# Top-2 mixture of experts behind a recurrent attention layer: combining, second normalisation and output by block instead of in a pass of their own

## The chip, the core and the metric

One core of a Trainium2 chip runs the whole kernel. The metric is the device time of one execution in microseconds (us): the median over several runs.

## The reference

`x` has two sequences of 2048 tokens with 256 channels, 4096 tokens in all.

```python
xx = pad(x, one step)[:, :-1, :]
k, v, r = (x*m + xx*(1-m)) @ W            # one m and W for each
a = (sigmoid(r) * wkv(decay, first, k, v)) @ Wo   # a scan over time in each channel
x1 = layernorm(x + a)
logits = x1 @ Wg + bg                     # 8 experts
s, e = top_k(logits, 2);  s = softmax(s)
h = act_e(x1 @ W1[e] + b1[e])             # 1024 wide; gelu for even e, silu for odd e
out = layernorm(x1 + sum over the two picks of s * (h @ W2[e] + b2[e]))
```

`wkv` keeps two running sums and a running maximum, so that exponentials stay bounded. All is fp32.

## The kernel before

The kernel is written engine by engine in Bass: each engine (PE, ACT, DVE, POOL, and SP for loads and stores) has a program of its own, and semaphores tie them together. An engine runs its instructions in the order in which they are written, so this order is what decides. Products of fp32 matrices are made as three products of a high and a low half ("h" and "l" in names).

**Attention stage.** Eight chunks of 256 time steps for both sequences (512 tokens, four groups of 128 rows). Each engine's `step(i)` works on several chunks: DVE scans chunk i, ACT makes its exponents (`exponents`, L885 to L890, `bonuses`, L895), and normalises chunk i-1 (`normalise_x1`, L933), for which POOL's `spread_of(i-1)` (four operations, L563 to L568) has made scale and shift. The router's choice is made by DVE in `choose` (maxima and their places, L1117 to L1130) and `place` (the slot of each pick in its expert's region, L1188 to L1199). POOL's `send_records` writes each token's record (x1 and two numbers, 258 floats) into `records_dram` twice, by eight indirect DMAs (L583), for chunk i-3, and ahead of `spread_of(i-1)`. SP stores x1 to `x1_dram`.

**Block stage.** The 8192 records lie in order of experts. They are worked through in blocks of 256 rows; for these inputs there are 35 in use, of at most 39. In step t, PE turns block t+2 (L823), makes product 1 of block t+1 into the four PSUM tiles `hT_ps` (L800) and product 2 of block t into `y_ps` (L809). ACT applies gelu or silu with the bias in place, writes the high half `aTh` and loads the records of a later block. DVE adds b2 (`y_sb`, L1299), makes the halves of x, the destination (`dest`, L1309) and the lower half `aTl` quarter by quarter (L1323). PE's product 1 of the block after next writes a quarter of `hT_ps` only when its `aTl` is done. POOL scatters the results by token and pick into `expert_out_dram` (L618, two a block). When the last block of expert e-2 is done it splits the weights of expert e from `staging` into `wx`: L533 rounds to the high half, L535 subtracts for the low half. Expert 1 is split before the first block.

**Last stage.** For 16 pieces of 128 time steps of both sequences, SP loads both picks' results of each token, DVE and ACT weigh and add them to x1, DVE makes mean and variance, POOL scale and shift (L634 to L639), ACT normalises (L1032), and SP stores to `out`.

A wait is written with a step's number: `t.upto(n)` stands for n increments in every step up to t, `t.upto(n, k)` for n in every step before t and k in step t; `after(engine, semaphore, value)` is left out where the value isn't positive. `t.slot` is the step's buffer in its ring.

Of the kernel before, what the change touches and what calls it, by code (L numbers as in the profile page):

```python
# [82 lines left out]
def build(nc, x, decay, first, mix_k, mix_v, mix_r, wkT, wvT, wrT, woT, w1, b1, w2, b2, wgT, bg, out):  # L83
# [18 lines left out]
    REC = C + 2  # L102
# [3 lines left out]
    PIECES = T // P  # L106
    RING = 4
    W1E, W2E = CC * F, FC * C
# [6 lines left out]
    ys = nc.dram_tensor("expert_out_dram", (2 * TOKENS, C), F32, kind="Internal").ap()  # L115
    x1d = nc.dram_tensor("x1_dram", (B, T, C), F32, kind="Internal").ap()

    with ExitStack() as ctx:
# [24 lines left out]
        top2 = sb("top2", [P, NCH, J, 2])  # L143
        score = sb("score", [P, NCH * J, 2])
        score_t = sb("score_t", [P, NCH * J, 2])
# [74 lines left out]
        slot_f = sb("slot_f", [P, J, 2], F32, phase_a)  # L220
        slot_i = [sb(f"slot_i{n}", [P, J * 2], I32, phase_a) for n in range(RECS)]
# [16 lines left out]
        xx = sb("xx", [P, PIECES, B, C])  # L238
# [3 lines left out]
        dest = [sb(f"dest{n}", [P, BH], I32, phase_b) for n in range(RING)]  # L242
# [4 lines left out]
        y_sb = [sb(f"y_sb{n}", [P, BH, C], F32, phase_b) for n in range(RING)]  # L247
# [4 lines left out]
        yy = [sb(f"yy{n}", [P, B, 2 * C]) for n in range(RING)]  # L252
        zz = [sb(f"zz{n}", [P, B, C]) for n in range(RING)]
        res = [sb(f"res{n}", [P, B, C]) for n in range(RING)]
        y2 = [sb(f"y2_{n}", [P, B, C]) for n in range(RING)]
        stats_c = [sb(f"stats_c{n}", [P, B, 6]) for n in range(RING)]
        mv_c = [sb(f"mv_c{n}", [P, B, 2]) for n in range(RING)]
        rstd_c = [sb(f"rstd_c{n}", [P, B]) for n in range(RING)]
        shift_c = [sb(f"shift_c{n}", [P, B]) for n in range(RING)]

# [3 lines left out]
        bias1_done, top2_done = sem("bias1_done"), sem("top2_done")  # L264
# [22 lines left out]
        x1_out = [sem(f"x1_out{n}") for n in range(RECS)]  # L287
# [6 lines left out]
        y_out = [sem(f"y_out{n}") for n in range(RING)]  # L294
# [3 lines left out]
        mm2_done, y_done = [sem(f"mm2_done{n}") for n in range(BH)], sem("y_done")  # L298
        exp_done, score_done = sem("exp_done"), sem("score_done")
        yy_in = [sem(f"yy_in{n}") for n in range(RING)]  # L300
        res_out = [sem(f"res_out{n}") for n in range(RING)]
        xx_in, y2_done, c_sum2 = sem("xx_in"), sem("y2_done"), sem("c_sum2")
        c_sum, c_bn, c_mv, c_var, c_rstd, c_res = (sem(n) for n in ("c_sum", "c_bn", "c_mv", "c_var", "c_rstd", "c_res"))

        REC_DMAS = 2 * J * 16
        ROUTE1, ROUTE2 = 2 * J + 3, 7
# [6 lines left out]
        def blocks_in_line(body):  # L313

            for n in range(-2, BLOCKS + 1):
                body(Step(None, n, RING, BLOCKS))

        LAST = ALWAYS // RING * RING

        def blocks(eng, body):  # L320

            plain = lambda n: Step(None, n, RING, BLOCKS)
            for n in range(-2, RING):
                body(plain(n))
            with eng.Fori(1, LAST // RING) as m:
                for n in range(RING):
                    body(Step(m, n, RING, BLOCKS, LAST // RING))
            for n in range(LAST, BLOCKS + 1):
                body(plain(n))
# [7 lines left out]

        def pieces(eng, body):

            for n in range(RING):  # L340
                body(Step(None, n, RING, PIECES))
            with eng.Fori(1, PIECES // RING) as m:
                for n in range(RING):
                    body(Step(m, n, RING, PIECES))

        def column(i, b, k):

            at = (i.off // TH * J + b * TH + i.off % TH) * 2 + k
            return at if i.fixed else i.m * (i.every // TH * J * 2) + at
# [15 lines left out]
        def store_chunk(sp, ap, i, rows, done):  # L365
            for b in range(B):
                sp.dma_start(ap[b, bass.ds(i.number * TC, TC), :].rearrange("(h p) c -> p h c", p=P), rows[:, b]).then_inc(done, 16)

# [9 lines left out]
        def kept(eng, c):  # L378

            after(eng, x1_out[c.number % RECS], c.number // RECS * B * 16)  # L380

        def phase_b_may_start(eng):
            eng.wait_ge(table_done, 1)
            for n in range(2):
                eng.wait_ge(dummy_out[n], 2 * 16)
            for n in range(RECS):
                eng.wait_ge(rec_out[n], users(n) * REC_DMAS)
                eng.wait_ge(x1_out[n], users(n) * B * 16)
# [17 lines left out]
        def _(sp):  # L406
# [26 lines left out]
            sp.wait_ge(padded, 3)  # L433
# [3 lines left out]
            def step(i):  # L437
# [24 lines left out]
            for e in range(2, E):  # L462
                sp.wait_ge(weights_ready, e)
                load_raw(e)
                if e == 2:
                    for b in range(B):
                        sp.dma_start(xx[:, :, b, :], x1d[b].rearrange("(q p) c -> p q c", p=P)).then_inc(xx_in, 16)
# [37 lines left out]
        def _(pool):  # L505
# [82 lines left out]
            def step(i):  # L588
# [6 lines left out]
                if (i - 1).exists:  # L595
                    spread_of(i - 1)
# [802 lines left out]
```

## Time and profile before

| | before |
|---|---|
| runs | 771.36, 774.31, 773.06 us; median 773.06 us |
| profiled execution | 775.2 us, its span 773.4 us |
| mean granted clock of TensorE | 0.907 |
| busy in the span: PE, DVE, ACT, POOL | 84%, 59%, 51%, 38% |
| longest groups: products L800 and L809 | 25% of the chain of waits each |
| DMA | 78.4 MB, 101 GB/s on average |

Times in the profile are microseconds from the span's start; a row of a timeline gives start, length, engine, line, operation, output and inputs, and in brackets how long the engine stood idle before it and what ended that. The chain of waits is followed back from the last instruction, at each step to what released it. Attention runs to about 290 us, blocks from there to 715 us, the last stage from there to the end.

### The profile page before, as it was taken

How to read it: one execution, taken by the hardware profiler on the slowest of the kernel's cores; microseconds unless marked ns; L12 is line 12 of the kernel's file. 1: busy time of each engine (PE TensorE's matmuls, PEld its weight loads, DVE VectorE, ACT ScalarE, POOL GpSimd, SP SyncE). 2: the span in 40 equal slices, each digit the busy share in tenths (PEclk: the TensorE clock that was granted, in tenths of full speed). 3: DMA queues.
4: the chain of work that ended last, by engine and by line, in shares of the span. 5: the costliest groups of instructions: out<-in, count | busy, mean ns of one | idle time of the engine just before them, and what ended most of it. 6: DMA issues, size and time to landing. Idle time of an engine off the chain costs nothing.

```text
span 773.4 us, 14741 instructions
## 1 busy us (share of the span) xinstructions
PE 648.2 (84%) x4512; PEld 605.9 (78%) x4512; DVE 453.3 (59%) x960; ACT 395.2 (51%) x717; POOL 295.3 (38%) x299
## 2 busy tenths in 40 slices
PE   4979799999976516999999999999999999999000
PEld 3858688788855416999999999999999999999000
DVE  3748889999996353844545345455464354442584
ACT  2545576576662103645546446456646546453374
POOL 4000116446555542525327263263461361212364
PEclk9998899999976657999999999999999999999555
DMA  8200221322122266661413214214141111201793
GB/s 262 80 28 1 81 82 56 111 81 99 67 75 97 91 176 206 198 228 39 152 51 115 86 43 151 58 33 153 50 159 49 39 46 43 57 12 34 232 309 123
DMA packets 56610, 78.39 MB, mean 101 GB/s; under 512 B 5174, under 2 KB 46083, under 8 KB 56356
## 3 DMA queue, kind: packets, MB, share of 16 engines
q1 hardware_dynamic: 40468, 50.54, 19.9%
q0 software_dynamic: 6496, 16.99, 6.3%
q10 hardware_dynamic: 9520, 9.25, 4.5%
q8 instruction: 71, 1.16, 0.6%
q14 instruction: 55, 0.45, 0.2%
HBM read 49.14 MB, written 28.40 MB: 100 GB/s over the span
## 4 chain that ended last, share of the span: by engine, by line
PE 73%; DVE 10%; issue 7%; ACT 3%; DMA 3%; POOL 2%; another core or an unknown queue 0%; SPq 0%; ACTq 0%; DVEq 0%; POOLq 0%
PE hT_ps L800 25%; PE y_ps L809 25%; PE vr_ps L670 8%; PE k_ps L670 7%; PE wo_ps L678 3%; PE xT_ps L823 2%; DVE o_all L1081 1%; DVE dest L1309 1%; PE small_ps L692 1%; POOL rstd_c L637 1%; PE xT_ps L661 1%; DVE xl L1159 1%; DMA yy<-expert_out_dram 1%; DMA records_dram<-rec,slot_i 1%; ACT res L1032 1%
## 5 line engine op out<-in xcount | busy, mean ns | idle before, releaser
L800 PE MATMUL hT_ps<-xTh,wx 128*128 128x256 f32 x1120 | 210.7, 286 | 0.4 <-issue 0.3
L809 PE MATMUL y_ps<-wx,aTh 128*128 128x256 f32 x1088 | 197.4, 283 | 0.9 <-DVE y_sb L1299 0.9
L800 PEld LDWEIGHTS hT_ps<-xTh,wx 128*128 128x128 f32 x1120 | 177.5, 192 | 1.3 <-issue 0.7
L1323 DVE TENSOR_TENSOR aTl<-hT_ps,aTh 128x512 fp32r<-128x512 f32 x140 | 93.3, 688 | 135.4 <-ACT aTh L991 135.4
L809 PEld LDWEIGHTS y_ps<-wx,aTh 128*128 128x128 f32 x1088 | 169.7, 192 | 1.1 <-issue 1.1
L618 POOL DMA_INDIRECT expert_out_dram<-y_sb,dest x70 | 68.3, 976 | 253.8 <-DVE y_sb L1299 239.0
L800 PE MATMUL hT_ps<-xTl,wx 128*128 128x256 f32 x560 | 158.7, 283 | 0.0
L809 PE MATMUL y_ps<-wx,aTl 128*128 128x256 f32 x544 | 154.0, 283 | 0.0
L985 ACT ACT_TABLE_LOAD x35 | 44.9, 1283 | 191.8 <-PE hT_ps L800 177.6
L985 ACT ACTIVATE hT_ps<-hT_ps,b_c 128x256 f32<-128x256 f32 x280 | 113.4, 469 | 0.8 <-PE hT_ps L800 0.3
L800 PEld LDWEIGHTS hT_ps<-xTl,wx 128*128 128x128 f32 x560 | 107.8, 192 | 0.0
L809 PEld LDWEIGHTS y_ps<-wx,aTl 128*128 128x128 f32 x544 | 104.4, 192 | 0.0
L583 POOL DMA_INDIRECT records_dram<-rec,slot_i x64 | 75.1, 1174 | 66.5 <-DVE rec L1199 40.6
L670 PE MATMUL vr_ps<-xh,wq 128*128 128x512 f32 x256 | 87.5, 414 | 0.0
L991 ACT ACTIVATE aTh<-hT_ps 128x512 fp32r<-128x512 f32 x140 | 84.2, 649 | 0.0
L1299 DVE TENSOR_TENSOR y_sb<-y_ps,b_b 128x256 f32<-128x256 f32 x70 | 29.4, 424 | 82.5 <-PE y_ps L809 81.2
L535 POOL TENSOR_TENSOR wx<-staging,wx 128x4096 fp32r<-128x4096 f32 x7 | 63.8, 9120 | 0.6
L670 PEld LDWEIGHTS vr_ps<-xh,wq 128*128 128x128 f32 x256 | 50.3, 197 | 11.8
L670 PE MATMUL k_ps<-xh,wq 128*128 128x512 f32 x128 | 48.0, 449 | 13.1 <-DVE nd L1088 11.1
L670 PE MATMUL vr_ps<-xl,wq 128*128 128x512 f32 x128 | 52.3, 408 | 0.0
L670 PEld LDWEIGHTS k_ps<-xh,wq 128*128 128x128 f32 x128 | 28.0, 219 | 21.1 <-issue 14.2
L678 PE MATMUL wo_ps<-wo,newton 128*128 128x256 f32 x128 | 34.9, 421 | 7.9 <-DVE newton L1109 4.4
(181 smaller groups left out, 870.0 us busy)
## 6 DMA issues: line engine op xcount, KB each, us to landing
staging<-in_L_ffn_W SPq DMA_DIRECT2D x16, 1024.0 KB
recs<-records_dram ACTq DMA_DIRECT2D x35, 258.0 KB
yy<-expert_out_dram SPq DMA_DIRECT2D x16, 512.0 KB, 5.3
xin<-in_L_attn_x SPq DMA_DIRECT2D x16, 256.0 KB, 4.4
xres<-in_L_attn_x SPq DMA_DIRECT2D x16, 256.0 KB, 3.0
x_dram<-rec SPq DMA_DIRECT2D x16, 256.0 KB, 3.3
xx<-x_dram SPq DMA_DIRECT2D x2, 2048.0 KB, 18.4
out<-res SPq DMA_DIRECT2D x16, 256.0 KB, 3.6
```

The costliest lines, as they stand in the source:

```text
L535: pool.tensor_tensor(wx[:, e % 2, 1, :], raw[:], wx[:, e % 2, 0, :].bitcast(F32), ALU.subtract).then_inc(weights_ready, 1)
L583: pool.indirect_dma_start(xs, bass.IndirectOffsetOnAxis(ap=slot_i[at][:, n:n + 1], axis=0), rec[at][:, j, :], None, bounds_check=DUMMY - 1 ...
L618: pool.indirect_dma_start(ys, bass.IndirectOffsetOnAxis(ap=dest[t.slot][:, h:h + 1], axis=0), y_sb[t.slot][:, h, :], None, bounds_check=2 ...
L670: ins = pe.matmul(out_ps.rearrange("p (b t) -> p b t", b=B), wq[:, mat, now, part, cc, oc * P:(oc + 1) * P], xpart[c.slot][:, cc, :, now:n ...
L678: ins = pe.matmul(wo_ps[:, h, :], mixed[:, cc, b, h * P:(h + 1) * P], wo[:, cc, :], start=cc == 0, stop=cc == CC - 1)
L800: ins = pe.matmul(hT_ps[b][:, f, :], wx[:, s, part, off:off + P], xpart[t.slot % 2][:, cc, :], start=k == 0, stop=k == len(terms) - 1)
L809: ins = pe.matmul(y_ps[h], apart[t.slot % 2][:, fc, h * P:(h + 1) * P], wx[:, s, part, off:off + C], start=k == 0, stop=k == len(terms) - 1)
L823: ins = pe.transpose(xT2_ps[:, cc, h * P:(h + 1) * P], recs[u.slot][:, h, cc * P:(cc + 1) * P], ident[:])
L985: act.activation(hT_ps[b][:, f, :], hT_ps[b][:, f, :], func, bias=b1_c[:, bass.ds(expert * FC + (2 * b + f), 1)]).then_inc(act_done, 1)
L991: act.activation(aTh[u.slot % 2][:, 2 * b - 2:2 * b, :], hT_ps[b - 1][:], ACT.Copy).then_inc(aTh_done, 1)
L1299: dve.tensor_tensor(y_sb[u.slot][:, h, :], y_ps[h], b2_b[:, bass.ds(expert * C, C)], ALU.add).then_inc(y_done, 1)
L1323: dve.tensor_tensor(aTl[u.slot % 2][:, 2 * b:2 * b + 2, :], hT_ps[b][:], aTh[u.slot % 2][:, 2 * b:2 * b + 2, :].bitcast(F32), ALU.subtract ...
```

## The change

The last stage is gone. Each record now carries all that its block needs: the token's number, the smaller and the larger of its two slots, two numbers that give the weight of either pick, and the smaller expert (262 floats). The weights come from POOL's new `compare` and `score_picks` and ACT's new `weigh` in the attention stage. A block's rows become `share = weight*(y + b2) + x1`, kept in SBUF and stored to `shares_dram`. For a row whose token had its other pick in an earlier block, that pick's share is fetched by an indirect load (`gather`); rows without one fetch nothing and read zeros. The weights are doubled, so the sum of both shares is twice the row to be normalised, and eps is taken times 4. The sum is normalised in the block stage and scattered to `out`, where rows that aren't the later pick have a number out of bounds. `shares_dram` and `other` are cleared first. x1 is neither stored nor reloaded. ACT's `normalise` is two Identity activations from `share` to `row_out`, and `store_shares` waits for `share_done` and issues one DMA of 256 KB.

```diff
@@ setup @@
-    REC = C + 2
+    REC = C + 6
+    KEEP = 6
+    MARKS = 8
-    ys = nc.dram_tensor("expert_out_dram", (2 * TOKENS, C), F32, kind="Internal").ap()
-    x1d = nc.dram_tensor("x1_dram", (B, T, C), F32, kind="Internal").ap()
+    us = nc.dram_tensor("shares_dram", (BLOCKS * BLK, C), F32, kind="Internal").ap()
@@ SP, step(i) of the attention stage @@
-                c = i - 2
-                if c.exists:
-                    store_chunk(sp, x1d, c, rec[c.number % RECS][:, :, 0:C].rearrange("p (b h) c -> p b h c", b=B), x1_out[c.number % RECS])
+                if i.exists:
+                    a, b = (BLOCKS * BH * n // NCH * P for n in (i.number, i.number + 1))
+                    sp.dma_start(us[a:b, :].rearrange("(n p) c -> p n c", p=P),
+                                 pad_rec[:, 0:C].unsqueeze(1).broadcast_to([P, (b - a) // P, C])).then_inc(shares_clear, 16)
@@ POOL, attention stage @@
+            def compare(c):
+                pool.wait_ge(route, c.upto(ROUTE1, 1 + 2 * J))
+                pool.tensor_tensor(gap[:], m8[:, :, 1], m8[:, :, 0], ALU.subtract).then_inc(gap_done, 1)
+                pool.wait_ge(later_done, c.upto(1))
+                pool.tensor_scalar(sign[:], later[:], -2.0, 1.0, ALU.mult, ALU.add).then_inc(gap_done, 1)
+            def score_picks(c):
+                at = c.number % RECS
+                pool.wait_ge(odds_done, c.upto(1))
+                pool.tensor_scalar(top_s[:], odds[:], 0.5, 0.5, ALU.mult, ALU.add).then_inc(score_done, 1)
+                pool.wait_ge(score_done, c.upto(7, 1))
+                pool.tensor_tensor(top_s[:], top_s[:], neg_one[:], ALU.pow).then_inc(score_done, 1)
...
             def send_records(c):
...
+                score_picks(c)
                 pool.wait_ge(label_done, c.upto(1))
+                pool.wait_ge(score_done, c.upto(7))
                 pool.wait_ge(x1_done, c.upto(J))
@@ POOL, step(i) @@
                 if early.exists and early.number < NCH - 3:
                     send_records(early)
+                if late.exists and late.number == NCH - 2:
+                    compare(late)
                 if (i - 1).exists:
                     spread_of(i - 1)
+                if late.exists and late.number != NCH - 2:
+                    compare(late)
@@ POOL, block stage @@
-            split(1)
+            def gather(t):
+                pool.wait_ge(where_done, t.upto(2))
+                if not t.fixed or t.number > 0:
+                    pool.wait_ge(share_out[(t.slot - 1) % RING], ring_count(t - 1, 16))
+                after(pool, sum_done, (t - RING).upto(1))
+                for h in range(BH):
+                    pool.indirect_dma_start(
+                        other[t.slot % RING][:, h, :], None, us,
...
             def scatter(t):
-                for e in range(2, E):
-                    with pool.If(end[e - 2] == t.number):
-                        split(e)
-                with if_used(pool, used, t):
-                    for h in range(BH):
-                        pool.wait_ge(y_done, t.upto(BH, h + 1))
-                        pool.indirect_dma_start(
...
+                pool.wait_ge(row_done, t.upto(BH))
+                for h in range(BH):
+                    pool.indirect_dma_start(
...
+                        row_out[t.slot % RING][:, h, :], None,
...
+            def block_step(t):
+                for stage, u in ((spread_z, t - 3), (gather, t - 1), (scatter, t - 4)):
+                    if u.exists:
+                        with if_used(pool, used, u):
+                            stage(u)
+                if t.exists and not (t.fixed and t.number == 0):
+                    for e in range(2, E):
+                        with pool.If(end[e - 2] == t.number):
+                            pool.wait_ge(share_done, (t - 1).upto(BH))
+                            split(e)
+            for n in range(MARKS):
+                block_step(Step(None, n, MARKS, BLOCKS))
+                if n == 1:
+                    split(1)
@@ PE, product 2 of block t @@
-                        after(pe, y_done, (t - 1).upto(BH))
+                        after(pe, share_done, (t - 1).upto(BH))
@@ ACT @@
+            def weigh(c):
+                act.wait_ge(gap_done, c.upto(2))
+                after(act, score_done, (c - 1).upto(7))
+                act.activation(odds[:], gap[:], ACT.Exp).then_inc(odds_done, 1)
@@ ACT, step(i), behind bonuses(i) @@
+                if (i - 3).exists and i.number < NCH:
+                    weigh(i - 3)
@@ ACT, block_step(t) @@
+                u = t - 4
+                        normalise(u)
                 u = t + 3
-                        after(act, txl_done, (u - RING).upto(1))
+                        after(act, share_done, (u - RING).upto(BH))
                         load_records(u)
...
+                u = t - 1
+                        store_shares(u)
@@ DVE, choose and place @@
+                dve.tensor_tensor(later[:], idxf[:, :, 1], idxf[:, :, 0], ALU.is_gt).then_inc(later_done, 1)
-                dve.tensor_copy(rec[c.number % RECS][:, :, C + 1:REC], slot_f[:, :, 1:2]).then_inc(slots, 1)
+                dve.tensor_tensor(rec[c.number % RECS][:, :, C + 1], slot_f[:, :, 0], slot_f[:, :, 1], ALU.min).then_inc(slots, 1)
...
@@ DVE, block stage @@
+            def shares(t):
...
+                    dve.tensor_tensor(y_ps[h], y_ps[h], b2_b[:, bass.ds(expert * C, C)], ALU.add).then_inc(y_done, 1)
+                    dve.scalar_tensor_tensor(out=share[at][:, h, :], in0=y_ps[h], scalar=weight[t.slot % 2][:, h:h + 1],
+                                             in1=recs[t.slot][:, h, 0:C], op0=ALU.mult, op1=ALU.add).then_inc(share_done, 1)
+            def add_other(t):
+                dve.wait_ge(other_in[t.slot], t.turn(16 * BH, 16 * BH))
+                dve.wait_ge(share_out[t.slot], t.turn(16, 16))
+                dve.tensor_tensor(share[at][:], share[at][:], other[t.slot][:], ALU.add).then_inc(sum_done, 1)
...
+                stages = [(shares, t - 1, ()), (halves, t + 2, ()), (add_other, t - 2, ()), (lower_quarter, t + 1, (0,)),
+                          (means, t - 2, ()), (mark, t, ()), (lower_quarter, t + 1, (1,)), (mark_more, t, ()),
+                          (lower_quarter, t + 1, (2,)), (mark_last, t, ()), (lower_quarter, t + 1, (3,))]
```

Three places where instructions move. DVE, one step of the block stage, before: the destinations (L1309) stand between the two halves of x, ahead of the four quarters of the lower half.

```order
L1299 TENSOR_TENSOR y_sb<-y_ps,b_b 128x256 x2
L336 COMPARE_AND_BRANCH
L1306 CAST xTh<-xT_ps 128x512
L1309 SCALAR_TENSOR_TENSOR dest<-recs,own_f 128x1 x2
L1314 TENSOR_TENSOR xTl<-xT_ps,xTh 128x512
L1303 UNCONDITIONAL_BRANCH
L336 COMPARE_AND_BRANCH
L1323 TENSOR_TENSOR aTl<-hT_ps,aTh 128x512 x4
```

The same step of the change, from the shares on: ten small operations of `mark`, `mark_more` and `mark_last` (L1344 to L1374) stand between the quarters (L1320).

```order
L1314 TENSOR_TENSOR xTl<-xT_ps,xTh 128x512
L1327 TENSOR_TENSOR share<-share,other 128x512
L1330 BN_STATS stats_z<-share 128x6 x2
L1320 TENSOR_TENSOR aTl<-hT_ps,aTh 128x512
L1337 BN_AGGR mv_z<-stats_z 128x2 x2
L1344 TENSOR_TENSOR mine<-recs,own_f 128x2
L1345 TENSOR_TENSOR first_e<-expert_no,recs 128x16
L1320 TENSOR_TENSOR aTl<-hT_ps,aTh 128x512
L1352 TENSOR_SCALAR far<-mine 128x2
L1353 TENSOR_TENSOR weight<-mine,recs 128x2
L1355 TENSOR_TENSOR first_e<-first_e,rowbase 128x16
L1320 TENSOR_TENSOR aTl<-hT_ps,aTh 128x512
```

POOL, the change's step of the block stage: the weight split (L478, L480) comes behind the small operations, two loads and two stores; before, it stood directly ahead of the two stores of a block.

```order
L592 TENSOR_TENSOR var_z<-mv_z,eps_b 128x2
L593 TENSOR_SCALAR neg_z<-mv_z 128x2
L595 TENSOR_TENSOR rstd_z<-var_z,half_neg 128x2
L597 TENSOR_TENSOR shift_z<-neg_z,rstd_z 128x2
L611 DMA other<-shares_dram,where_to 128x256 x2
L620 DMA out<-row_out,where_to 4096x256 x2
L632 COMPARE_AND_BRANCH
L478 TENSOR_SCALAR wx<-staging 128x4096
L480 TENSOR_TENSOR wx<-staging,wx 128x4096
```

POOL, the change's step of the attention stage: the seven operations of `score_picks` (L526 to L538) stand between the record's label (L543) and the eight sends (L555), and so ahead of `spread_of` (L508).

```order
L543 IOTA rec 128x4
L526 TENSOR_SCALAR top_s<-odds 128x4
L528 TENSOR_TENSOR top_s<-top_s,neg_one 128x4
L530 TENSOR_TENSOR low_s<-odds,top_s 128x4
L532 TENSOR_TENSOR lead<-top_s,low_s 128x4
L534 TENSOR_TENSOR shift_s<-lead,later 128x4
L536 TENSOR_TENSOR rec<-lead,sign 128x4
L538 TENSOR_TENSOR rec<-low_s,shift_s 128x4
L555 DMA records_dram<-rec,slot_i 35072x262 x8
L508 TENSOR_TENSOR var_e<-mv,eps_b 128x4
```

Here the sends of a chunk come seven operations later than before, and with them all that POOL does for the chunk two behind.

## Rows read from the trace of the kernel before

**Rows 1.** Page, part 4: the chain of waits by engine
```profile
PE 73%; DVE 10%; issue 7%; ACT 3%; DMA 3%; POOL 2%; another core or an unknown queue 0%; SPq 0%; ACTq 0%; DVEq 0%; POOLq 0%
```

**Rows 2.** Windows (start:end length, PE, PEld, DVE, ACT, POOL busy (x), PEclk, DMA share, GB/s)
```profile
109.56:136.20 26.64, 25.97 (x135) 21.65 (x134) 25.34 (x57) 17.73 (x25) 13.78 (x15) 1.00 0.31 100
320.00:715.10 395.10, 394.12 (x3292) 393.48 (x3292) 181.82 (x332) 207.95 (x430) 143.86 (x81) 1.00 0.27 86
715.10:773.40 58.30, 0.00 (x0) 0.00 (x0) 36.63 (x113) 30.54 (x64) 26.59 (x65) 0.52 0.67 221
```

**Rows 3.** Chain of waits in the block stage: start us, us, what
```profile
356.11 5.75 PE hT_ps L800 x48
368.05 5.75 PE hT_ps L800 x48
```

**Rows 4.** ACT in one block (start us, us, ...), and L1323 from the page
```profile
381.54 1.28 ACT L985 ACT_TABLE_LOAD   x1 [5.67 <-PE hT_ps L800]
382.84 1.54 ACT L985 ACTIVATE hT_ps<-hT_ps,b_c 128x256 f32<-128x256 f32 x4
L1323 DVE TENSOR_TENSOR aTl<-hT_ps,aTh 128x512 fp32r<-128x512 f32 x140 | 93.3, 688 | 135.4 <-ACT aTh L991 135.4
```

**Rows 5.** DVE and POOL at L1309, two weight splits and the set-up
```profile
309.50 6.54 DVE dest L1309
...
453.56 3.63 POOL L533 TENSOR_SCALAR wx<-staging 128x4096 fp32r<-128x4096 f32 x1
457.27 9.12 POOL L535 TENSOR_TENSOR wx<-staging,wx 128x4096 fp32r<-128x4096 f32 x1
...
464.26 2.29 DVE L1309 SCALAR_TENSOR_TENSOR dest<-recs,own_f 128x1 int32<-128x1 f32 x2
...
11.45 0.93 POOL L400 TENSOR_SCALAR r<-newton,consts_c 128x256 f32<-128x256 f32 x2
...
12.04 1.42 DVE L1050 TENSOR_TENSOR wq<-den,wq 128x1024 fp32r<-128x1024 f32 x1
13.50 1.23 DVE L1050 TENSOR_TENSOR wq<-r,wq 128x1024 fp32r<-128x1024 f32 x1
```

**Rows 6.** Attention chunk 4: ACT, DVE and POOL timelines
```profile
139.68 1.07 ACT L885 ACTIVATE B<-nd 128x1024 f32<-128x1024 f32 x1 [1.15 <-DVE nd L1088]
...
143.49 1.32 ACT L895 ACTIVATE bonus<-nd,consts_c 128x512 f32<-128x512 f32 x2
...
145.77 2.29 DVE L1147 TENSOR_TENSOR_SCAN q_all<-A,B 128x1028 f32<-128x1028 f32 x1
...
154.40 1.25 DVE L1174 TENSOR_TENSOR num<-num,gate 128x1024 f32<-128x1024 f32 x1
...
147.09 1.75 POOL L583 DMA_INDIRECT records_dram<-rec,slot_i  x1 [0.30 <-issue]
...
156.94 0.97 POOL L583 DMA_INDIRECT records_dram<-rec,slot_i  x1 [0.30 <-issue]
158.43 0.20 POOL L563 TENSOR_TENSOR var_e<-mv,eps_b 128x4 f32<-128x4 f32 x1 [0.52 <-issue]
...
159.99 0.21 POOL L568 TENSOR_TENSOR shift<-neg_mean,rstd 128x4 f32<-128x4 f32 x1
```

**Rows 7.** ACT after the last exponents, and PE's waits from 236 to 290
```profile
219.88 1.05 ACT L885 ACTIVATE B<-nd 128x1024 f32<-128x1024 f32 x1
239.20 2.07 ACT L933 ACTIVATE rec<-xres,shift,rstd 128x256 f32<-128x256 f32 x4 [4.68 <-POOL shift L568]
PE wo_ps L678 <- DVE newton L1109: 2.8, 1, 2.8
```

**Rows 8.** POOL in the last normalising step, and the page's out store
```profile
764.63 0.19 POOL L634 TENSOR_TENSOR var_e<-mv_c,eps_b 128x2 f32<-128x2 f32 x1
765.83 0.20 POOL L639 TENSOR_TENSOR shift_c<-neg_mean,rstd_c 128x2 f32<-128x2 f32 x1
out<-res SPq DMA_DIRECT2D x16, 256.0 KB, 3.6
```

More of the change, by code:

```diff
@@ L220, in build @@
         slot_f = sb("slot_f", [P, J, 2], F32, phase_a)
+        gap, odds, later, sign, top_s, low_s, lead, shift_s = (
+            sb(n, [P, J], F32, phase_a) for n in ("gap", "odds", "later", "sign", "top_s", "low_s", "lead", "shift_s"))
         slot_i = [sb(f"slot_i{n}", [P, J * 2], I32, phase_a) for n in range(RECS)]
@@ L313, in blocks_in_line @@
         def blocks_in_line(body):
-            for n in range(-2, BLOCKS + 1):
+            for n in range(-2, BLOCKS + 4):
                 body(Step(None, n, RING, BLOCKS))
[L318 to L329, printed above, removed]
         def blocks_in_use(eng):
@@ L993, in _, with store_shares, normalise @@
             used = blocks_in_use(act)
+            def store_shares(t):
+                act.wait_ge(share_done, t.upto(BH))
+                act.dma_start(us[t.number * BLK:(t.number + 1) * BLK, :].rearrange("(h p) c -> p h c", p=P),
+                              share[t.number % KEEP][:]).then_inc(share_out[t.slot], 16)
+            def normalise(t):
+                act.wait_ge(rstd_z_done, t.upto(1))
+                after(act, out_done[t.slot], t.turn(16 * BH))
+                for h in range(BH):
+                    act.activation(row_out[t.slot][:, h, :], share[t.number % KEEP][:, h, :], ACT.Identity,
+                                   bias=shift_z[t.slot][:, h:h + 1], scale=rstd_z[t.slot][:, h:h + 1]).then_inc(row_done, 1)
             def block_step(t):
+                u = t - 4
+                if u.exists:
+                    with if_used(act, used, u):
+                        normalise(u)
                 u = t + 3
@@ new lines, in means, with mark @@
+            def means(t):
+                dve.wait_ge(bn_z, t.upto(BH))
+                after(dve, rstd_z_done, (t - RING).upto(1))
+                take_wait(dve)
+                for h in range(BH):
+                    dve.bn_aggr(mv_z[t.slot][:, h, :], stats_z[t.slot][:, h, :]).then_inc(mv_z_done, 1)
+            def mark(t):
+                n = t.slot % 2
+                rows = recs[t.slot]
+                dve.wait_ge(rec_in[t.slot], t.turn(16, 16))
+                dve.tensor_tensor(mine[n][:], rows[:, :, C + 2], own_f[:, t.number, :], ALU.is_equal).then_inc(mine_done, 1)
+                dve.tensor_tensor(first_e[n][:], expert_no[:].unsqueeze(1).broadcast_to([P, BH, E]),
+                                  rows[:, :, C + 5:C + 6].broadcast_to([P, BH, E]), ALU.is_equal).then_inc(base_done, 1)
```

348 lines of the change are left out of this document (148 added, 200 removed).

## The prediction

> **What bounds the kernel now.** I read the chain of waits by engine first: PE holds 73% of it [rows 1]. Then the stretches. An attention chunk takes 26.64 us, with PE busy for 25.97 and DVE for 25.34 of them: both are nearly full [rows 2]. In the block stage PE is busy for 394.1 of 395.1 us, DVE for 182 and ACT for 208; behind it stand 58.30 us without PE [rows 2]. The pieces of the chain give a block step: one product starts at 356.11, the same of the next block at 368.05, so a step is 11.95 us [rows 3]. I call the start of such a step S, its PE order being transposes (0.44), product 1 (5.75), product 2 (5.76). Per block ACT is busy for 208/33 = 6.3 us and DVE for 5.5 [rows 2]. One switch of ACT's function table takes 1.28 us, and the next activation starts 1.30 after the switch began [rows 4].
>
> The row that matters most is one that the shares hide. `dest` (L1309), a DVE operation of one column, normally takes 0.2 us. Under the first weight split it held the chain for 6.54 us, and under a later split it took 2.29 [rows 5]: it ends at 466.55, the POOL operation that started at 457.27 and takes 9.12 at 466.39. Its inputs both lie in SBUF. So a DVE operation that reads two SBUF operands doesn't run beside POOL's. The split's first half (L533, 3.63) seems to do the same: L1050 took 1.42 beside POOL's last scaling, which ends at 12.38, and 1.23 free [rows 5]. The lower halves aTl read PSUM and SBUF and take 0.69 on average over 140 [rows 4], so they aren't held. The other way round, POOL's second send took 1.75 beside DVE's scans where a free one takes 0.97 [rows 6].
>
> **Part 1, attention stage: +26.** Per chunk the change adds an exponential on ACT, 9 small POOL operations and three DVE ones (3 x 0.17 less a copy); it drops one store to DRAM and adds a clearing store of 1.3 MB. DMA engines are busy for 0.31 of this stretch [rows 2], which hides both stores; were they not hidden, the loads of the next chunk would come late. What counts is that seven of the POOL operations are in sequence and stand *ahead of* the eight sends of chunk i-3, which stand ahead of the four operations that ACT's `normalise_x1` waits for; ACT's next exponents stand behind that.
> - Let E be the start of the exponents, 139.68. ACT ends `bonuses` at 144.81 = E+5.1 [rows 6]; `weigh` adds 0.3.
> - Seven POOL operations free: 2.6, from the four that run from 158.43 to 160.20, a power among them, and 0.27 for each of three more. But from 145.77 to 155.65 DVE runs two-SBUF operations nearly back to back (two scans, denominator, bonus, numerator, gate; first and last in [rows 6]). If each POOL operation gets one turn between two of them, the chain ends with the last but one, about E+14.6, and so costs 9.2 and not 2.6.
> - Then first send 0.9 later, eight sends 10.0 (1.28 apart, free now since DVE's long row is over), 0.5, four operations 1.8 [rows 6], `normalise_x1` 2.07 [rows 7], two copies of v 1.1: E+31.0. A chunk takes 26.64 today, so the loop sets the pace: +4.3 in each of chunks 3 to 6, **+17.2**. With the free chain it is E+24.4, and nothing is lost.
> - Behind the last exponents (E = 219.88) `normalise_x1` of chunk 6 starts at 239.20, E+19.3 [rows 7]; after the change at E+27.8: **+8.5**. Of it 2.8 is slack, since chunk 7's output product waits 2.8 for DVE there [rows 7], and chunk 6's records wait for their own score chain, +2.7: +8.4 together. Part 1 is +25.6, rounded to **+26**; low end +2.7 (that last chain alone).
>
> **Part 2, block stage: +40.** `shares` adds two DVE operations (0.45 each), `add_other` one of 0.7, statistics 1.0, and ten marks of 0.2: 5.5 + 5.1 = 10.8 in a slot of 11.95. ACT gets a second table load (1.28), the normalising pair (1.1, half of the four of `normalise_x1`) and one DMA issue (0.4): 6.3 + 2.8 + 0.4 = 9.5. Both fit, so PE still sets the step; product 2 now waits for `share_done` and not `y_done`, 0.45 later, which matters in the last block alone (+0.5), since product 1 lies between elsewhere.
> Where it doesn't fit is the splits. POOL's step is now spread (1.4), gather, scatter, split. The gather of block t-1 waits for the store of share t-2; ACT issues that at S+8.7 of the step before (behind its last activation), and a store of that size lands in 3.6 [rows 8]: S+0.3. Two gathers and two scatters at 0.9 + 4 x 1.28 end at S+6.05. So the split runs from S+6.15, its long half from S+9.8 to S+19.15 (now from S+2.3, ending at S+15.2). `mark` (two SBUF inputs, DVE at about S+6.9) is held by it, with what is queued behind: the lower halves 1 to 3 that PE needs from S+12.39+1.44 = S+13.84 on, because product 1 of the next block overwrites their PSUM. `mark`'s first operation gets through between the two halves, the second after S+19.15; the lower half ends at S+19.95, PE's three remaining quarters and a little at S+24.7, where product 2 was due at S+18.15. Loss 6.5 for each of six splits: **+39**. Split 1, moved behind the first gather, loses 2.8 where it loses 2.4 now: +0.4. Part 2 is 39 + 0.4 + 0.5 = **+39.9**. If L533 doesn't hold DVE, marks get past before S+9.8 and nothing is lost, or only the last of them is caught (4 to 5 us): the low end is 2.5 for each split, +15.9 with the rest. I take the upper one, because both of rows 5 point at it.
> The Trainium skill ("SBUF - State Buffer", section "Who interferes with whom") says the same of two-SBUF operations and POOL's reads; but it infers that `tensor_tensor` leaves descriptor writing alone. By that rule sends aren't lengthened, which the 1.75 beside DVE's scans contradicts; the sum would not change, since my late sends run free.
>
> **Part 3, the tail: -39.8.** It is 58.30 now [rows 2]. After PE's last product: b2 and weight 0.95, store issue 0.4 and landing 3.6 (+4.95); sum 0.7, statistics 1.0 (+6.6); POOL's four small operations take 1.40 free (764.63 to 766.03) [rows 8] (+8.0); table 1.28 and normalising 1.09 (+10.4); two scatters, 0.9 and 1.28 (+12.6); landing 3.6; closing 2.3. That is 18.5, so 58.3 - 18.5 = **39.8** saved. The bound from below, landing in 2.3: 17.2.
>
> **Sum:** 775.2 + 26.0 + 39.9 - 39.8 = 801.3 for the profiled execution, which lies 2.1 above the median of the runs (773.06). So the median becomes **799**.
>
> **Rivals.**
> - *Faster, the tail wins.* The POOL chain slips between DVE's operations, and the marks pass ahead of the split: 775.2 + 2.7 + 15.9 - 39.8 = 754.0, median **752** (745 to 760). For it: POOL's sends are only lengthened by 0.3 to 0.9, never blocked. Against: `dest` waits for a whole POOL operation in all seven splits. 22%.
> - *Chain cheap, splits dear*: 801.3 - 23.3 = 778.0, median **776**. 8%.
> - *Chain dear, splits cheap*: 801.3 - 24.0 = 777.3, median **775**. 10%.
> - *The share's round trip or DVE passes its slot in each block.* DVE at 10.8 of 11.95 has 1.15 to spare; if gather's data come later than `add_other`'s place at S+2.4, everything behind it in DVE's queue moves. It decides from 1.2 us of lateness on; one us over, 35 times, +35, of which the split losses absorb some: **830**. 7%.
> - *ACT passes its slot.* It has 11.95 - 9.5 = 2.45 to spare and two table switches in each block. Should each cost one load again (1.28), ACT needs 12.0, with hand-overs about 12.25: 35 x 0.3 = 10, **809**. Against it: the 1.30 of rows 4. 5%.
> The Trainium skill ("ScalarE: Activation LUTs", "What ACT_TABLE_LOAD costs") gives 1283 ns for the load, as here, and about 1380 ns of drain on top for each switch. By that rule this last rival would hold; the 1.30 from the load's start to the next activation leaves no room for a drain behind it, though the load shown follows an idle engine.
>
> **How the numbers follow.** The forecast has 48%. A measurement of this kernel can tell a change of about 0.5% from none: below 769.2 is faster, above 776.9 slower. Slower: 48 + 7 + 5, and 5 of the two middle rivals, 65%. Faster: 22 + 3 of these, 25%. Same: the other 10%. The forecast's own range is 790 to 808, from a few us in the chain's end and the split's start. The range for 8 in 10 goes from 748 to 812: it leaves out the lower third of the first rival and the 7% at 830, with the edges of the forecast.
>
> **What would show it.** Right: DVE's `mark` or the first operation behind it lasting until POOL's L480 ends, near S+19, in six blocks, with PE gaps of 5 to 7 us there; POOL's L526 to L538 spread over 9 us; exponents 31 us apart from chunk 3 on; a tail of some 18 us. Wrong: L526 to L538 within 3 us and chunks of 27; splits without a gap on PE; block steps above 12 us everywhere, which would point at ACT or the share's round trip.

## The result, and the profile after

The changed kernel takes 816.41 us (median; runs from 814.79 to 817.01), the kernel before 773.68 on the same chip: a ratio of 1.0535, 95% interval 1.051 to 1.056. The direction was right, and the size was not: I had 799, and 812 as the upper end. The profiled execution took 816.4 us, its span is 814.6, its mean granted clock 0.89. I cut both spans at PE's first block transposes and PE's last product. One execution of the kernel with both orders (754.76 us, see below) was 2% slower than its fastest, and its number below leaves that one out.

| stretch | before | after | difference | predicted |
|---|---|---|---|---|
| attention, to PE's first transposes of a block | 294.97 | 318.12 | +23.2 | +26.0 |
| block stage, to PE's last product | 420.13 | 474.89 | +54.8 | +39.9 |
| tail | 58.30 | 21.59 | -36.7 | -39.8 |
| span | 773.4 | 814.6 | +41.2 | +26.1 |

The windows of the changed kernel, with the columns of [rows 2]:

```profile
318.12:793.01 474.89, 423.02 (x3452) 418.28 (x3452) 343.36 (x863) 295.50 (x551) 269.85 (x280) 0.93 0.29 89
793.01:814.60 21.59, 0.00 (x1) 0.00 (x0) 4.24 (x12) 7.12 (x9) 12.81 (x18) 0.58 0.21 69
```

In the block stage PE is now busy for 423 of 475 us, and the granted clock is 0.93, where it was 1.00 from 320 us on [rows 2]. PE's waits in it (engine, line, releaser: us in all, times, longest):

```profile
PE hT_ps L804 <- DVE aTl L1320: 48.4, 12, 7.3
```

One of the six splits, first on POOL, then on DVE (start, length, engine, line):

```profile
500.30 3.64 POOL L478 TENSOR_SCALAR wx<-staging 128x4096 fp32r<-128x4096 f32 x1
504.02 8.86 POOL L480 TENSOR_TENSOR wx<-staging,wx 128x4096 fp32r<-128x4096 f32 x1
```

```profile
502.01 1.95 DVE L1344 TENSOR_TENSOR mine<-recs,own_f 128x2 f32<-128x2 f32 x1
503.88 0.16 DVE L1345 TENSOR_TENSOR first_e<-expert_no,recs 128x16 f32<-128x16 f32 x1
503.96 0.68 DVE L1320 TENSOR_TENSOR aTl<-hT_ps,aTh 128x512 fp32r<-128x512 f32 x1
504.57 8.34 DVE L1352 TENSOR_SCALAR far<-mine 128x2 f32<-128x2 f32 x1
```

These answer to [rows 5]. `mine` is held by the first half of the split until 503.94, as L1050 seemed to be. Then both marks and one lower half slip in, and `far` is held until 512.88, the end of the second half. The chain of waits shows what PE makes of it:

```profile
480.11 5.66 PE hT_ps L804 x48
485.77 5.46 PE y_ps L813 x48
491.23 0.44 PE xT_ps L827 x4
491.67 5.66 PE hT_ps L804 x48
497.32 2.75 PE y_ps L813 x24
504.57 8.34 DVE far L1352
513.72 5.49 PE hT_ps L804 x24
```

After the wait, 24 matmuls take 5.49 us where a whole 48 take 5.66 otherwise. The windows of the wait and of what follows it show why:

```profile
506.10:513.70 7.60, 0.28 (x3) 0.07 (x1) 7.60 (x6) 0.00 (x0) 7.52 (x4) 0.73 0.00 0
513.70:519.20 5.50, 5.48 (x25) 5.48 (x26) 5.15 (x15) 0.18 (x1) 3.70 (x6) 0.50 0.98 322
```

PE stood idle for 7.3 us, and then ran at a granted clock of 0.50, the lower of its two levels (1.2 GHz), for these 5.5 us. The lower level lasts 3.2 to 6.2 us past the end of the wait in the six split steps; as half of such a time is lost, that is 15.8 us in all. The six split steps, from one product 1 to the next, take 22.53, 20.62, 22.28, 22.22, 22.55 and 21.67 us, 10.4 on average above a plain step. A plain step takes 11.55 or 11.75 us, and took 11.95 before: something got faster, too.

In the attention stage, the score chain of chunk 1 on POOL, with the exponents started at 143.73:

```profile
149.03 1.10 POOL L526 TENSOR_SCALAR top_s<-odds 128x4 f32<-128x4 f32 x1 [5.86 <-ACT odds L911]
150.21 2.93 POOL L528 TENSOR_TENSOR top_s<-top_s,neg_one 128x4 f32<-128x4 f32 x1
153.22 0.88 POOL L530 TENSOR_TENSOR low_s<-odds,top_s 128x4 f32<-128x4 f32 x1
...
156.60 1.18 POOL L538 TENSOR_TENSOR rec<-low_s,shift_s 128x4 f32<-128x4 f32 x1
158.66 1.10 POOL L555 DMA_INDIRECT records_dram<-rec,slot_i  x1 [0.88 <-POOL rec L538]
```

It takes 8.75 us and ends at E+14.1, and the first send starts at E+14.9; in [rows 6] the second one already starts at E+7.4. The exponents of this chunk stand 33.8 us behind those before them, and the later ones 31.1 to 31.3 us apart:

```profile
175.04 1.05 ACT L889 ACTIVATE B<-nd 128x1024 f32<-128x1024 f32 x1
...
206.35 1.05 ACT L889 ACTIVATE B<-nd 128x1024 f32<-128x1024 f32 x1
...
237.44 1.04 ACT L889 ACTIVATE B<-nd 128x1024 f32<-128x1024 f32 x1
```

The last ones start at 237.44, against 219.88 in [rows 7]: +17.6. From the last chunk without a score chain ahead of its sends it is more: those exponents start at 109.9, against 113.0 before, so four chunks take 127.5 where they took 106.9: +20.6.

### The profile page after: what moved, and what is told of

It is laid out like the page before. It is cut to its first block, busy times and chain, and to the rows that moved or that the text cites. A ratio compares the mean times of both kernels' runs of the same rounds, so it can differ in the third digit from the quotient of the medians.

```text
span 814.6 us, 14940 instructions
## 1 busy us (share of the span) xinstructions
PE 655.8 (81%) x4512; PEld 609.2 (75%) x4512; DVE 570.8 (70%) x1384; ACT 446.4 (55%) x763; POOL 444.7 (55%) x524
## 4 chain that ended last, share of the span: by engine, by line
PE 38%; issue 16%; DVE 16%; POOL 13%; ACT 11%; ACTq 3%; DMA 1%; DVEq 1%; POOLq 0%; SPq 0%
PE hT_ps L804 16%; PE y_ps L813 12%; DVE far L1352 6%; POOL records_dram L555 5%; PE k_ps L674 4%; ACT hT_ps L996 4%; PE vr_ps L674 3%; DVE aTl L1320 2%; POOL top_s L528 2%; ACT aTh L1002 2%; DVE share L1306 2%; DVE y_ps L1304 1%; PE xT_ps L827 1%; DVE o_all L1085 1%; POOL top_s L526 1%
## 5 line engine op out<-in xcount | busy, mean ns | idle before, releaser
L804 PE MATMUL hT_ps<-xTh,wx 128*128 128x256 f32 x1120 | 223.6, 295 | 48.9 <-DVE aTl L1320 48.4
L804 PEld LDWEIGHTS hT_ps<-xTh,wx 128*128 128x128 f32 x1120 | 186.2, 200 | 52.5 <-DVE aTl L1320 51.1
L813 PE MATMUL y_ps<-wx,aTh 128*128 128x256 f32 x1088 | 190.6, 279 | 1.4 <-DVE share L1306 1.4
L1320 DVE TENSOR_TENSOR aTl<-hT_ps,aTh 128x512 fp32r<-128x512 f32 x140 | 96.5, 690 | 113.5 <-ACT aTh L1002 101.9
L804 PE MATMUL hT_ps<-xTl,wx 128*128 128x256 f32 x560 | 163.2, 291 | 0.0
L611 POOL DMA_INDIRECT other<-shares_dram,where_to x70 | 74.9, 1071 | 121.8 <-DMA shares_dram<-share 82.5
L804 PEld LDWEIGHTS hT_ps<-xTl,wx 128*128 128x128 f32 x560 | 112.4, 201 | 0.0
L620 POOL DMA_INDIRECT out<-row_out,where_to x70 | 74.0, 1057 | 22.7 <-issue 20.7
L555 POOL DMA_INDIRECT records_dram<-rec,slot_i x64 | 67.9, 1061 | 24.2 <-issue 17.1
L480 POOL TENSOR_TENSOR wx<-staging,wx 128x4096 fp32r<-128x4096 f32 x7 | 62.2, 8881 | 0.6
L674 PEld LDWEIGHTS vr_ps<-xh,wq 128*128 128x128 f32 x256 | 49.9, 195 | 11.7
L1352 DVE TENSOR_SCALAR far<-mine 128x2 f32<-128x2 f32 x35 | 54.6, 1561 | 0.1
L941 ACT ACTIVATE rec<-xres,shift,rstd 128x256 f32<-128x256 f32 x32 | 16.6, 590 | 65.1 <-POOL shift L513 65.1
```

The costliest lines, as they stand in the source:

```text
L480: pool.tensor_tensor(wx[:, e % 2, 1, :], raw[:], wx[:, e % 2, 0, :].bitcast(F32), ALU.subtract).then_inc(weights_ready, 1)
L555: pool.indirect_dma_start(xs, bass.IndirectOffsetOnAxis(ap=slot_i[at][:, n:n + 1], axis=0), rec[at][:, j, :], None, bounds_check=DUMMY - 1 ...
L611: pool.indirect_dma_start(other[t.slot % RING][:, h, :], None, us, bass.IndirectOffsetOnAxis(ap=where_to[t.slot][:, 1, h:h + 1], axis=0), ...
L620: pool.indirect_dma_start(out.rearrange("b t c -> (b t) c"), bass.IndirectOffsetOnAxis(ap=where_to[t.slot][:, 0, h:h + 1], axis=0), row_ou ...
L674: ins = pe.matmul(out_ps.rearrange("p (b t) -> p b t", b=B), wq[:, mat, now, part, cc, oc * P:(oc + 1) * P], xpart[c.slot][:, cc, :, now:n ...
L804: ins = pe.matmul(hT_ps[b][:, f, :], wx[:, s, part, off:off + P], xpart[t.slot % 2][:, cc, :], start=k == 0, stop=k == len(terms) - 1)
```

## Experiments

All ratios are to the kernel before, run beside.

**Marks first.** DVE's ten marks go ahead of `add_other`.

```diff
-                stages = [(shares, t - 1, ()), (halves, t + 2, ()), (add_other, t - 2, ()), (lower_quarter, t + 1, (0,)),
-                          (means, t - 2, ()), (mark, t, ()), (lower_quarter, t + 1, (1,)), (mark_more, t, ()),
-                          (lower_quarter, t + 1, (2,)), (mark_last, t, ()), (lower_quarter, t + 1, (3,))]
+                stages = [(shares, t - 1, ()), (halves, t + 2, ()), (mark, t, ()), (mark_more, t, ()), (mark_last, t, ()),
+                          (add_other, t - 2, ()), (lower_quarter, t + 1, (0,)), (means, t - 2, ()),
+                          (lower_quarter, t + 1, (1,)), (lower_quarter, t + 1, (2,)), (lower_quarter, t + 1, (3,))]
```

> The changed kernel with the ten marks on DVE ahead of add_other and the first lower half, so that they are done before POOL's weight split starts. Theory (POOL's split holds the marks, and with them the lower halves PE waits for; PE then runs at half clock for a while): the six steps of 20.6 to 22.6 us fall to ordinary ones of 11.6 to 12.0, -60 us or so, 756 (750 to 766). Rival (the split steps are long because POOL as a whole is late, its gathers and scatters after the split feeding DVE and ACT late): the long steps shrink by less than half, over 785. If PE's steps return from 11.55 to 11.95 where PE never stalls, it is 765 and not 756.

Measured: 761.5 us, ratio 0.986 (0.981 to 0.990). The same work in another order is 55 us faster than the changed kernel. PE's waits for the lower halves fall from 48.4 to 4.6:

```profile
PE hT_ps L804 <- DVE aTl L1320: 4.6, 2, 2.8
```

The marks are still held, but later, when nobody waits for them:

```profile
481.19 9.05 POOL L480 TENSOR_TENSOR wx<-staging,wx 128x4096 fp32r<-128x4096 f32 x1
```

```profile
480.89 1.29 DVE L1320 TENSOR_TENSOR aTl<-hT_ps,aTh 128x512 fp32r<-128x512 f32 x2 [0.52 <-ACT aTh L1002]
...
485.54 4.72 DVE L1344 TENSOR_TENSOR mine<-recs,own_f 128x2 f32<-128x2 f32 x1
```

Plain steps stay at 11.55 to 11.78 although PE hardly stalls any more, so their speed isn't due to the stalls.

**Scores early.** The seven score operations run at the end of POOL's step, one step ahead of their sends, and `weigh` behind `normalise_x1`.

```diff
@@ POOL, send_records(c) and the end of step(i) @@
-                score_picks(c)
+                if c.number >= NCH - 3:
+                    score_picks(c)
...
+                if late.exists and late.number < NCH - 3:
+                    score_picks(late)
@@ ACT, step(i) @@
-                if (i - 3).exists and i.number < NCH:
-                    weigh(i - 3)
...
-                if i.number == NCH - 1:
+                if (i - 2).exists and i.number < NCH:
                     weigh(i - 2)
```

> The changed kernel with the seven score operations at the end of POOL's step, one step earlier than the sends, in a stretch in which DVE reads no two SBUF operands, and their exponential behind normalise_x1. Theory (the score chain, stretched to 8.8 us by DVE, sets the loop of the chunks): the exponents are 26.7 to 27.2 apart again and not 31.3, and the last sends end some 21 us earlier: 795 (790 to 800). Rival (the added work itself, or the clearing stores, makes the chunks long): stays within 3 us of 816.

Measured: 802.5 us (797.2 to 805.4), ratio 1.038 (1.034 to 1.043). In the profile of its fastest run (span 795.5) the exponents are 27.0, 28.8, 27.6 and 27.2 us apart, and the first transposes come at 300.33 and not 318.12, 17.8 earlier. The loop of the chunks was the chain's. One chain still meets DVE's row of two-SBUF operations, and in each of four chunks the first send starts beside that row and takes 3.3 to 3.4 us where a free one takes 0.97, so a part of the expected 21 is left. The median gained 13.9.

**Both of these together.**

> Marks first and scores early together. If both causes are independent the gains add: 816 - 60 - 21 = 735 (728 to 748), faster than the kernel before (773). If one of them only uncovers the other's wait, it stays above 755.

Measured: 740.8 us (739.1 to 747.7), ratio 0.960 (0.953 to 0.966): faster than both kernels. Added up, the two measured gains of 54.9 and 13.9 give 747.6. So they add within the spread of the runs, and the two orders alone turn the change from 5% slower to 4% faster. That spread has a source in the attention stage, which the profiles show: with the same order there, the exponents of the last chunks are 28.8, 27.6 and 27.2 us apart in scores early, and 30.2, 29.5 and 29.0 in the kernel with the late load below. What sets which of the two comes up wasn't tried.

**Store first.** ACT issues `store_shares(t - 1)` right behind the load of the records, ahead of the activations.

```diff
                         load_records(u)
+                u = t - 1
+                        store_shares(u)
                 u = t + 1
...
-                u = t - 1
-                        store_shares(u)
```

> The changed kernel with ACT storing the shares of block t-1 ahead of the activations of block t+1 instead of behind them. Theory (the split starts at S+9.1 and not S+6 because the gather waits for a store that ACT issues 6.5 us late): the split starts 2.5 to 3 us earlier, PE's wait of 7.3 falls to about 4.6, six times: 800 (795 to 806). Rival (the split's start is set by something else, such as the shares of block t-1): unchanged, 814 to 818.

Measured: 830.5 us, ratio 1.073 (1.068 to 1.077): my theory of this step fell. The six splits start 8.8 to 9.0 us behind product 1's start, and 7.8 to 9.9 in the changed kernel: no earlier, since the gather now waits for the marks (`where_to`, 26 times) and not for the store. And the DMA issue stands ahead of the activations:

```profile
385.37 0.38 ACTq L987 DMA_DIRECT2D recs<-records_dram  x1
385.79 1.64 ACTq L1008 DMA_DIRECT2D shares_dram<-share  x1
388.36 1.28 ACT L996 ACT_TABLE_LOAD   x1 [4.71 <-issue]
```

This is one of the longest; most of these issues take 0.48. From the load's issue to the table load it is 1.7 to 3.1 us in the blocks, where it was 1.2 to 1.6. Plain steps become 11.6 to 12.6 us. ACT has idle time in each, but not in this loop: shares of t-1 on DVE, then the load that waits for them, then the activations of t+1, the lower halves, the shares of t. In the changed kernel it takes 11.7 us from one block's shares (481.88) to the next one's (493.59), a whole step, so whatever lengthens it lengthens each step.

**Load late.** ACT's load of the records, with its wait for the shares, goes behind the activations. Alone, and on top of both orders:

```diff
-                u = t + 3
-                        after(act, share_done, (u - RING).upto(BH))
-                        load_records(u)
                 u = t + 1
...
+                u = t + 3
+                        after(act, share_done, (u - RING).upto(BH))
+                        load_records(u)
```

> The changed kernel with ACT's load of the records of block t+3, which waits for the shares of block t-1, behind the activations of block t+1 instead of ahead of them. Theory (this wait ties ACT's activations to DVE's shares in a loop that takes about one step of 11.55, so that DVE and the split run some 3 us later against PE than I had reckoned, and a DMA issue of 0.4 more in it cost 14 us): activations start 3 us earlier against PE, the six splits begin nearer S+6, PE waits 3 to 4 us and not 7.3 in each, and the half clock behind it shrinks: 816 - 18 to 24 = 795 (788 to 805). Rival (the loop is not what puts the split so late): the split steps stay above 20 us. A cost on the other side: the records may come up to 0.5 us late in each step, +15 at most.

> Marks first, scores early, and the load of the records behind the activations. Where the marks are not held, nothing waits for the split, so the loop has no stall to shorten: 740 to 746, as both. If the loop still costs something in the steps of 13 to 14.6 us, up to 8 less.

Measured: 833.8 us, ratio 1.075 (1.069 to 1.081), and 829.2, ratio 1.070 (1.065 to 1.075). PE's waits in the first of them, which show two things at once:

```profile
PE xT_ps L827 <- DMA recs<-records_dram: 45.1, 20, 19.7
PE hT_ps L804 <- DVE aTl L1320: 17.0, 6, 4.1
```

The wait for held lower halves fell from 48.4 to 17.0 us, and split steps to 15 to 20 us. The six splits start 5.4 to 6.0 us behind product 1's start, where the changed kernel has 7.8 to 9.9 and I had reckoned 5.7: this is what the theory of the loop has. It isn't a clean test, since all steps are longer here and that alone gives the marks more room. The 19.7 in the first row is the wait before the first block (20.3 in the changed kernel). But the records, whose load leaves some 5 us later against product 1, miss PE's transposes in most steps, which then take some 13.4 us. I had put that at 0.5 a step, and it is 1.5 to 2; where nothing was to be gained, it costs 88 us.

**Lag 3.** Both orders, with normalising and scatter of block t-3 in step t.

```diff
-                u = t - 4
+                u = t - 3
                         normalise(u)
...
-                for stage, u in ((spread_z, t - 3), (gather, t - 1), (scatter, t - 4)):
+                for stage, u in ((spread_z, t - 3), (gather, t - 1), (scatter, t - 3)):
```

> Marks first and scores early, with a block normalised and scattered three steps behind and not four. Theory (the tail of 21.6 us against my 18.5 is POOL working off four blocks' scatters and scales one after another): one pair of scatters less in the tail, -2.5 us against both, 739 to 743 where both had 742. Rival (the tail is the latency of the last block's share, gather and sum): no difference.

Measured: 785.9 us, ratio 1.015 (1.011 to 1.020), 45 us over the kernel it was made from. The tail is 23.0 us (784.4 less the last product's end at 761.4), no shorter. This doesn't decide for the rival: with four steps of lag the tail is anything from 18.7 to 21.8 us in the profiles of these kernels, a spread of more than the 2.5 asked for. The part on why the prediction was wrong says what goes with it. What costs is this, in ACT's timeline of a split:

```profile
383.64 1.09 ACT L1016 ACTIVATE row_out<-share,shift_z,rstd_z 128x256 f32<-128x256 f32 x2 [11.40 <-POOL shift_z L600]
384.33 0.38 ACTq L988 DMA_DIRECT2D recs<-records_dram  x1
```

ACT stands 11.4 us in front of `normalise`, which waits for POOL's four small operations, which stand behind the split. Behind it are the loads, and PE waits up to 7.4 us for records. The fourth step of lag was the cover of the split.

**Where the tiles lie.** Five kernels ask why PE's plain step is 11.95 before and 11.55 to 11.75 after. An unused tile moves the tiles behind it: 32 KB a partition in the first, 64 bytes apiece in the next three, 192 bytes in the last.

```diff
@@ marks first @@
+        spacer = sb("spacer", [P, 16, B, C])
         phase_b = ExitStack()
@@ before: both, the first alone, the second alone @@
+        spacer0 = sb("spacer0", [P, 16])
         raw = sb("staging", [P, WE])
...
+        spacer1 = sb("spacer1", [P, 16])
         xx = sb("xx", [P, PIECES, B, C])
@@ the changed kernel @@
+        spacer = sb("spacer", [P, 48])
         phase_b = ExitStack()
```

> Marks first, with an unused tile of 32 KB a partition ahead of the block stage's tiles, where the kernel before had the reloaded x1. It asks why a block step of PE without any wait takes 11.55 to 11.75 here and 11.95 before. If it is where the tiles lie in SBUF: steps of 11.95, 761 + 10 = 771. If not: 758 to 765, as marks first.

> The kernel before, with two unused tiles of 64 bytes a partition, one ahead of the staged weights and one ahead of the block stage's tiles, so that weights and block tiles lie at the same offsets within 256 bytes as in the changed kernel. It asks why PE's block step without a wait takes 11.95 us before and 11.55 to 11.75 in every version of the changed kernel. If it is where the operands lie: steps of 11.55 to 11.75, 763 (759 to 768). If not: 11.95 and 771 to 776.

> The kernel before with the first of the two tiles alone: weights and block tiles move together by 64 bytes. If it is the offset between the two operands that counts, steps of 11.95; if it is where each lies, they change.

> The kernel before with the second of the two tiles alone: the block tiles move by 64 bytes against the weights. If the offset between the two counts, steps of 11.55 to 11.75; if not, 11.95.

> The changed kernel with an unused tile of 192 bytes a partition ahead of the block stage's tiles, so that weights and block tiles have the same offset within 256 bytes, as in the kernel before. If the change owed part of its time to the offset: plain steps of 11.95 and not 11.55 to 11.75, some 28 of them 0.2 to 0.4 longer, 816 + 8 = 824 (820 to 829). If the offset matters only in the kernel before: 814 to 818.

Measured, with the address within 256 bytes at which the weights (`wx`) and the block tiles that PE multiplies them with (`xTh` to `aTl`) begin:

| kernel | weights, tiles | us | plain step |
|---|---|---|---|
| before | 128, 128 | 774.0 | 11.95 |
| before, both spacers | 192, 0 | 761.4; ratio 0.984 (0.980 to 0.989) | 11.55, 11.75 |
| before, all moved | 192, 192 | 775.1 (one run) | 11.95 |
| before, tiles moved | 128, 192 | 762.6 (one run) | 11.55, 11.75 |
| marks first | 192, 0 | 761.5 | 11.55 to 11.78 |
| marks first, 32 KB on | 192, 0 | 762.7 | 11.55 to 11.85 |
| changed | 192, 0 | 816.4 | 11.55, 11.75 |
| changed, same offset | 192, 192 | 820.3; ratio 1.061 (1.057 to 1.065) | 11.95 |

The chain of waits of the kernel before with its tiles moved, against 5.75 for product 1 in [rows 3]:

```profile
377.57 5.45 PE hT_ps L801 x48
```

Where both operands of the products begin at the same offset, 48 matmuls take 5.75 us; 64 bytes apart they take 5.45 to 5.66. The kernel before gains 11 to 13 us by 64 bytes that nobody uses. The change moved the tiles apart by chance, and this hid some of its cost.

## Why the prediction was wrong, point by point

- **Attention, +26 predicted, +23.2 measured: right in mechanism and nearly in size.** The chain ends at E+14.1 (E+14.6), chunks are 31.3 apart (31.0), the last exponents come 17.6 later (17.2). The near hit of 17.6 is in part luck: the first of the four chunks took 33.8 and not 31.0, so the four cost 20.6, but the profiled execution was 3.1 us ahead of the one before when they began. The profiles of all these kernels put that point between 109.9 and 113.0, and the two compared lie at the ends. Without this head start the stage costs 26.3. Moving the chain gave 17.8 back in one profile.
- **The block stage is where it failed: +39.9 predicted, +54.8 measured.** The mechanism stands: the split holds the marks, the marks hold the lower halves, and PE waits; marks first took the waits away. The failing step is "Loss 6.5 for each of six splits". It is 10.4 over a plain step of 11.55 us, for two reasons. The larger is a term that I put at nothing: PE lost its clock. The lower level costs 2.6 in each split on average, 15.8 in all. The sign of it was on record, a granted clock of 0.52 in the stretch without PE [rows 2], and I gave it no price. The smaller is the wait, 7.3 (6.4 in one split) and not the 6.1 from S+13.84 to S+19.95, since the split ran from S+9.1 (500.30 against 491.23) and not S+6.15. There I reckoned ACT's activations at their old place, S+2.0 (381.54 in [rows 4], where S is 379.56), and overlooked a wait that the change adds: the load of the records now waits for the shares of the block before, ahead of the activations. In the step with S = 479.68 they start at S+6.0, and the store that the gather waits for is issued at S+11.3 and not S+8.7:

```profile
484.40 0.38 ACTq L987 DMA_DIRECT2D recs<-records_dram  x1
485.69 1.28 ACT L996 ACT_TABLE_LOAD   x1 [3.02 <-issue]
491.00 0.38 ACTq L1008 DMA_DIRECT2D shares_dram<-share  x1
```

Only the first of the three lower halves got through in exchange. Against the old step of 11.95 the six splits cost 60.2 us, and the other steps gave 5.4 back.
- **Two slips in the sums of Part 2.** ACT's 6.3 + 2.8 + 0.4 counts the DMA issue twice (9.1, not 9.5). DVE's parts add up to 4.6 and with 5.5 to 10.1, not 10.8. Measured in the plain step from 479.68, ACT is busy for 8.48 us and DVE for 7.98. That both fit was right; the rival of ACT's slot leaned on the 9.5.
- **What I left out on the other side:** the plain steps are 0.2 to 0.4 shorter by the new place of the tiles. The spacer that takes this back costs the changed kernel 4 us in the median, less than the 8 I expected there, since the waits shrink with it: its six split steps sum to 127.4 us and not to 131.9. So the reordered work alone would have been worse still.
- **The tail, 21.6 and not 18.5.** I reckoned with latencies one after another and POOL free. The chain of waits runs through POOL's instructions from 793.72 to the last scatter. The last scatter starts 16.9 us behind the last product, where I had 12.6; what follows it takes 4.7 and not 5.9 (3.6 of landing and 2.3 of closing, and no row shows the 2.3 by itself). The wait comes from a load that my path left out, the last gather, which starts only behind a pair of scatters and four small operations of older blocks:

```profile
793.72 1.12 POOL L611 DMA_INDIRECT other<-shares_dram,where_to  x1 [0.80 <-issue]
799.29 0.72 DVE L1327 TENSOR_TENSOR share<-share,other 128x512 f32<-128x512 f32 x1 [3.48 <-DMA other<-shares_dram,where_to]
```

Behind the sum, ready at 801.2, the four small operations start at 803.50, behind a pair of scatters, and the block's own scatter at 808.61 behind another. Where the last pair of gathers starts before the last product ends, the tail comes near my 18.5: 2.0 us before it in scores early (tail 18.9), 3.6 before it in store first (18.7), against 0.7 behind it here. Load late lies between (1.0 before, tail 20.9). No edit moved the gather alone, so this is read from profiles and not tested.
- The rivals: neither chain nor split was cheap. The rival of the table switches did not come about: in a plain step PE waits for nothing, and two switches fit. A load right behind an activation, at 491.98, is followed by the next activation at 493.28, 1.30 later, as in [rows 4]. The rival of the slot was nearer than its 7%: the loop of DVE and ACT lasts a whole step, and an edit that put one DMA issue into it cost 14 us.
- The 1.75 of a send stands beside scans, and a send also reads its slots from SBUF. So the row shows that a send can be held, and not that the inference about `tensor_tensor`, which the prediction says it contradicts, is wrong.

The Trainium skill ("SBUF - State Buffer", section "Who interferes with whom") lets `tensor_scalar` contend with GpSimd in its two-port modes; here `far`, one SBUF input of 2 elements a partition, was held for 8.34 us. That is consistent with the row; no run here tells the mode.

## What to carry to other kernels

A long operation of POOL on SBUF (3.6 and 8.9 us here) held DVE's next operation with two SBUF inputs, and everything queued behind it: put such small operations where nobody waits for what follows them, here ahead of the lower halves. Where PE is the bound, price a stall of several microseconds with the slow clock behind it, which here added a third. And a lag between stages, or a load issued early, can be the cover of a rare long operation: look at what waits in that case before shortening it.

## What was not expected of the hardware

- A DVE operation with one SBUF input (`far`, [128x2]) is held as well: 8.34 us, to the end of POOL's L480. Lower halves, which read PSUM and SBUF, are not (0.68 in the same stretch).
- After 6.4 to 7.3 us without matmuls PE ran at a granted clock of 0.50 for another 3.2 to 6.2 us, in each of the six splits.
- The offset between the two operands of a matmul counts: 119 to 120 ns apiece at the same offset within 256 bytes, 114 to 118 at 64 bytes' difference, 11 to 13 us of 774 in the whole kernel. Moving both together changed nothing (775.1, one run). Which offsets are good beyond the ones in the table wasn't tried.
